# A transformer block on one core: every engine's parts put in another order, laid out with VectorE and GpSimd excluding each other

## The chip, the cores and the metric

The kernel runs on one core of a Trainium2 chip. The metric is the device time of one execution in microseconds. Before the change the median of three runs is 976.28 us (975.53 to 977.0). Engines are called by their short names: PE is TensorE (matmul), PEld its weight load, DVE VectorE, ACT ScalarE, POOL GpSimd, SP the engine that issues the DMAs.

## The reference

Sixteen sequences of 256 tokens with 128 features each pass through one block, all in float32. Cut to its steps:

```python
x = x + layernorm(attn_ref(layernorm(x)))   # 1: selective scan, an MLP, causal attention, an MLP
x = x + layernorm(ffn_ref(layernorm(x)))    # 2: gated feed-forward, hidden size 512
# attn_ref, for each sequence
vg = rms_norm(x) @ in_proj_w; value = silu(conv4(vg[:256])); gate = vg[256:]
Bm, Cm = x @ B_proj_w, x @ C_proj_w                   # 16 heads x 64
y = selective_scan(value, A, Bm, Cm, dt) + D * value  # decay of each head to the power (q - k)
x = x + (y * silu(gate)) @ out_proj_w;  x = x + relu(rms_norm(x) @ fc)**2 @ proj
q, k, v = ...; rms_norm and rope on q and k; softmax(q k / sqrt(8), causal) @ v   # 16 heads, 4 for k and v
x = x + att @ o_w;  x = x + relu(rms_norm(x) @ fc)**2 @ proj
# ffn_ref
h = silu(x @ w1) * (x @ w2); h = gelu(h @ h1); h = gelu(h @ h2); return h @ w3
```

## The kernel before

The program is written engine by engine. The work of one sequence `i` is cut into named parts, and each part is a small Python function that first waits for semaphores, then issues one to 48 instructions, and then raises its own semaphore. `PER` says how many instances of a part a sequence has. Sequences overlap: while one is in its scan, an earlier one is in attention and one before that in the feed-forward. Nothing is decided at run time. `ORDERS` (L48) is a table with one list of part names for each engine, `run` walks it, and each engine executes its list strictly in that order, so a part whose input is late holds up all that stands behind it on its engine.

The parts of PE and their instructions as the profile shows them: `tin` (transposes of `xm` and `X`), `inv` and `gat` (`w_in`), `bc` (`w_B`, `w_C`, eight of a sequence), `cb` (`BC` by `BC`, eight), `v` (`M,xpad`, four), `vt` (transposes of `val`), `out` (`w_out`), `up` and `down` (`w_mfc`, `w_mpj`), `t3` and `qkv` (`xa`, `w_qkv`), `qt`, `kt` (`Qs`, `Ks`), `s` (`KT,QT`), `mt` (`Mh`), `e` (`QT,KT`), `pv` (`PT,Va`), `yt`, `t4`, `o`, `t5`, `upb`, `downb` (`w_apj`), `t6`, `w1` and `w2` (`x6H`, `x6L`), `h1` and `h2` (`gH`, `gL` by `w_h`; 24 matmuls each instance, two of each), `w3` (`w` by `gAB`). Products that need float32 precision are split in a high and a low half (`xnH` and `xnL`, `x6H` and `x6L`, `gH` and `gL`).

Three forms of PE work matter below. Most parts use the array's 128 rows and 128 columns. `cb` works on 64 rows at a time (`64*128` in the profile). `v` and `pv` fill 32 columns each (`128*32`), `s` and `e` use 32 rows (`32*128`).

Around PE stand these parts. DVE: `nrm` (`X<-xm`, L932), `xnlo` (`xnL`, L937), `conv` (`val<-vpad`, L949 and L951), `m` (`M<-pool,LM`, L961 and L962), `nw`, `rp`, `qs` (normalisation and rope of q and k, L994 to L1057), `mx` (`mneg`, L1064), `mh`, and the layernorms. ACT: `bcx` (PSUM to `BC`), `ex` (exponential to `PT`), the activations. POOL: `sel` (the causal mask on `PT`), `sq` and `sqb` (squares), `glo` and `hlo` (low halves of the feed-forward), `xr`, and small powers `r1` to `r8`. The setup, once: `pex` on ACT and `plm` on DVE make the decay table `LM` (L579, L852); `plo` on DVE makes the low halves of `w_in`, `w_B`, `w_C` (L862, L865); `fsc` and `flo` on POOL scale and split the weights of the feed-forward (L414, L419, ten each of 128x512); `fold` on DVE folds scales into weights. The first `relu` waits for six `flo`, since `hid` holds raw weights until then.

PSUM has eight banks. `BANKS` gives each PE part its bank or banks, and `claim` waits for the part that last read a bank.

Of the kernel before, what the change touches and what calls it, by code (L numbers as in the profile page):

```python
# [1510 lines left out]
```

## Time and profile before

| | |
|---|---|
| median of 3 runs | 976.28 us |
| the profiled execution | 976.42 us, its span 974.7 us, mean granted clock 0.988 |
| PE busy | 888.5 us (91%), 9248 matmuls |
| DVE busy | 667.8 us (69%) |
| ACT busy | 578.2 us (59%) |
| POOL busy | 460.0 us (47%) |

The span runs from the first to the last instruction; 1.7 us of the profiled execution lie outside it. A busy share says how much an engine works, not whether its work is waited for. The page's chain of work that ended last is 64% PE, 22% DVE, 7% issue, 3% ACT, 2% POOL.

### The profile page before, as it was taken

What the parts mean: (1) busy time and instruction counts of PE and PEld (TensorE: products, weight loads), DVE (VectorE), ACT (ScalarE), POOL (GpSimd) and SP (SyncE); (2) the same over time, 40 slices, a digit from 0 to 9 for tenths busy, and PEclk for the clock granted to TensorE, in tenths of its full rate; (3) what the DMA queues carried; (4) which work ended last, traced back from release to release, by engine and by line L of the source; (5) the groups of instructions that cost most, each with busy time, mean ns of one, the idle gap of its engine ahead of it and who ended that gap; (6) DMA issues with size and microseconds to landing.
All of it is one profiled execution on the core that took longest, in us unless ns stands there. A gap on an engine that the chain in (4) does not pass through costs nothing.

```text
span 974.7 us, 24913 instructions
## 1 busy us (share of the span) xinstructions
PE 888.5 (91%) x9248; PEld 758.0 (78%) x9248; DVE 667.8 (69%) x1803; ACT 578.2 (59%) x1220; POOL 460.0 (47%) x708
## 2 busy tenths in 40 slices
PE   0689989999999999998999999999999999989785
PEld 0667768787979888987878898888877887878575
DVE  5978969866777767758576884875776686746320
ACT  3644365766747557746565768567475575575532
POOL 1574344625543637435345545355263644463432
PEclk9999999999999999999999999999999999999899
DMA  8100000000000000000000000000000000000000
GB/s 280 59 17 7 7 7 2 7 1 13 7 13 7 13 2 7 13 12 6 12 7 2 17 2 12 8 12 7 12 2 2 2 13 1 13 1 13 12 3 9
DMA packets 17926, 15.71 MB, mean 16 GB/s; under 512 B 2064, under 2 KB 15760, under 8 KB 17552
## 3 DMA queue, kind: packets, MB, share of 16 engines
q1 hardware_dynamic: 17808, 14.12, 4.6%
q8 instruction: 76, 1.25, 0.5%
q14 instruction: 42, 0.34, 0.1%
HBM read 12.02 MB, written 2.10 MB: 14 GB/s over the span
## 4 chain that ended last, share of the span: by engine, by line
PE 64%; DVE 22%; issue 7%; ACT 3%; POOL 2%; DMA 1%; SPq 0%; POOLq 0%; DVEq 0%; ACTq 0%
PE pool L1170 59%; PE pool L1187 5%; DVE mneg L1064 2%; DVE val L951 2%; DVE M L961 1%; DVE M L962 1%; ACT PT L726 1%; DVE W L1018 1%; DVE val L949 1%; DVE gAB L1144 1%; DVE W L1020 1%; POOL PT L496 1%; DMA X<-in_x 1%; DVE LM L852 1%; DVE val L968 1%
## 5 line engine op out<-in xcount | busy, mean ns | idle before, releaser
L1064 DVE TENSOR_REDUCE mneg<-pool 128x2 f32<-128x512 f32 (+1 forms) x192 | 119.0, 683 | 54.7 <-PE pool L1170 54.7
L1170 PE MATMUL pool<-gH,w_h_hi 128*128 128x256 f32 x512 | 149.1, 291 | 4.8 <-POOL gL L542 2.2
L1170 PE MATMUL pool<-gL,w_h_hi 128*128 128x256 f32 x512 | 143.8, 281 | 0.0
L1170 PE MATMUL pool<-gH,w_h_lo 128*128 128x256 f32 x512 | 143.8, 281 | 0.0
L961 DVE TENSOR_TENSOR M<-pool,LM 128x512 f32<-128x512 f32 x128 | 87.6, 685 | 55.2 <-PE pool L1170 54.8
L726 ACT ACTIVATE PT<-pool 128x512 f32<-128x512 f32 x192 | 99.2, 603 | 31.8 <-PE pool L1170 31.5
L1170 PE MATMUL pool<-BC 64*128 64x256 f32 (+1 forms) x1024 | 111.4, 345 | 3.3 <-ACT PT L726 1.7
L496 POOL TENSOR_SCALAR_AFFINE_SELECT PT<-PT 128x256 f32<-128x256 f32 (+1 forms) x192 | 89.2, 488 | 42.4 <-ACT PT L726 39.0
L1170 PEld LDWEIGHTS pool<-BC 64*128 64x128 f32 x1024 | 87.6, 187 | 26.1 <-issue 14.1
L644 ACT ACTIVATE BC<-pool 128x512 f32<-128x512 f32 x128 | 75.6, 603 | 54.2 <-PE pool L1170 50.9
L1170 PEld LDWEIGHTS pool<-gH,w_h_hi 128*128 128x128 f32 x512 | 96.9, 189 | 7.2 <-issue 3.2
L1170 PEld LDWEIGHTS pool<-gL,w_h_hi 128*128 128x128 f32 x512 | 97.0, 189 | 0.2
L1170 PEld LDWEIGHTS pool<-gH,w_h_lo 128*128 128x128 f32 x512 | 96.8, 189 | 0.0
L542 POOL TENSOR_TENSOR gL<-gAB,gH 128x512 fp32r<-128x512 f32 x32 | 41.3, 1301 | 65.2 <-ACT gH L787 64.9
L547 POOL TENSOR_TENSOR gL<-gAB,gH 128x512 fp32r<-128x512 f32 x32 | 41.0, 1286 | 50.1 <-ACT gH L801 50.0
L1170 PE MATMUL pool<-M,xpad 128*32 128x256 f32 (+1 forms) x1024 | 54.8, 332 | 3.6 <-DVE M L962 3.6
L1170 PE MATMUL pool<-PT,Va 128*32 128x128 f32 (+1 forms) x1024 | 53.2, 338 | 5.1 <-POOL PT L496 5.1
L806 ACT ACTIVATE gAB<-pool 128x512 f32<-128x512 f32 x32 | 19.1, 598 | 63.5 <-PE pool L1170 63.4
L951 DVE SCALAR_TENSOR_TENSOR val<-vpad,cols,val 128x256 f32<-128x256 f32 x96 | 54.9, 612 | 0.4
L962 DVE TENSOR_TENSOR M<-pool,LM 128x256 f32<-128x256 f32 x128 | 53.0, 414 | 0.0
L1170 PE MATMUL pool<-xnH,w_B_hi 128*128 128x256 f32 x128 | 44.0, 344 | 4.4 <-DVE M L962 3.9
L512 POOL TENSOR_TENSOR hid<-hid 128x512 f32<-128x512 f32 x32 | 33.5, 1051 | 29.7 <-ACT hid L766 29.7
(235 smaller groups left out, 2428.0 us busy)
## 6 DMA issues: line engine op xcount, KB each, us to landing
X<-in_x SPq DMA_DIRECT2D x16, 128.0 KB, 2.1
x<-in_x SPq DMA_DIRECT2D x16, 128.0 KB, 2.2
out<-ob SPq DMA_DIRECT2D x16, 128.0 KB, 2.1
hid<-in_w_h SPq DMA_DIRECT2D x1, 1024.0 KB, 8.9
gAB<-in_w_h SPq DMA_DIRECT2D x1, 1024.0 KB, 9.4
PT<-in_w_B SPq DMA_DIRECT2D x1, 512.0 KB, 4.9
PT<-in_w_C SPq DMA_DIRECT2D x1, 512.0 KB, 6.4
Qs<-in_s SPq DMA_DIRECT2D x1, 512.0 KB, 5.0
```

The source lines that it names most:

```text
L496: g.affine_select(w, w, pattern=[[0, w.shape[1]], [1, P]], compare_op=ALU.is_ge, fill=0.0, base=0, channel_multiplier=-1).then_inc(S["sel" ...
L512: g.tensor_tensor(h, h, h, ALU.mult).then_inc(S["sqb"], 1)
L542: g.tensor_tensor(gL[:, J], gA[:, J], gH[:, J].bitcast(F32), ALU.subtract).then_inc(S["glo"], 1)
L547: g.tensor_tensor(gL[:, J], gB[:, J], gH[:, J].bitcast(F32), ALU.subtract).then_inc(S["hlo"], 1)
L644: a.activation(BC[:, n % NBC, :], bank("bc", i, k), ACT.Copy).then_inc(S["bcx"], 1)
L726: a.activation(PT[:, n % NPT, :], bank("e", i, k // 4, k % 4), ACT.Exp).then_inc(S["ex"], 1)
L951: last = v.scalar_tensor_tensor(dst, vpad[:, b, k:k + L], w, dst, ALU.mult, ALU.add)
L961: v.tensor_tensor(M[:, n % NM, :, 0:L], pool8[:, b:b + 2, 0:L], LM[:, 2 * k:2 * k + 2, :], ALU.mult)
L962: v.tensor_tensor(M[:, n % NM, :, L:3 * P], pool8[:, b:b + 2, L:3 * P], LM[:, 2 * k:2 * k + 2, 0:P], ALU.mult).then_inc(S["m"], 1)
L1064: v.reduce_max(dst, o, axis=AX.X, negate=True).then_inc(S["mx"], 1)
L1170: return p.matmul(o, lhsT, rhs, start=start, stop=True, skip_group_check=True)
L1187: last = p.transpose(o[:, k * P:(k + 1) * P], src(k), ident[:])
```

## The change

All five lists of `ORDERS` and the table `BANKS` are replaced. The lists hold the same parts, the same number of each: no operand, shape or buffer changes. By its description the new order was laid out with DVE and POOL excluding each other wherever a DVE instruction has all its inputs in SBUF. One wait is added, on POOL in `xr`, for POOL's own part of the sequence before. Two lines are added, so every line after it stands two higher in the kernel after.

```diff
 ORDERS = dict(
     PE=(
-        "tin inv gat bc bc bc cb cb cb bc bc bc vt v cb cb bc v cb cb bc v cb tin v inv bc gat bc cb cb out bc bc bc vt t2 cb "
...
+        "tin inv bc bc bc gat bc bc cb cb bc bc cb cb vt bc v v cb cb cb cb v v tin bc inv out t2 up up bc bc bc down bc cb "
...
     DVE=(
-        "st0 dec ag0 st0 ag0 xh m01 dec xh dec plo dec xm dec plo dec nrm plo plm plm plm plm plm plm plm plm xnlo fold fold "
...
 BANKS = (
-    "0102314523016745023451234512312301234501231045123450230245234502012321024501236745012301452672014567201456201745"
...
+    "0102304567012345670124567014530123230230145204523674516730450267450360724523701745021374650127426375012567126735"
...
@@ -464,6 +464,8 @@
                 pool.wait_ge(S["xh"], at("xh", i))
                 g.tensor_tensor(xr[:, i % 2], xh[:, i % 2], by(R_A1), ALU.mult).then_inc(S["xr"], 1)
             elif k == 1:
+                if i >= 1:
+                    pool.wait_ge(S["xr"], at("xr", i - 1))
                 pool.wait_ge(S["xm2"], at("xm2", i))
                 g.tensor_tensor(xt[:], xm[:, i % 2], by(R_A0), ALU.mult).then_inc(S["xr"], 1)
```

What the tables do is seen in the instructions. The start on DVE, before, from the first `nrm` (`X<-xm`) on:

```order
L932 TENSOR_SCALAR X<-xm,rsd 128x128 x2
L865 TENSOR_TENSOR w_C_lo<-PT,w_C_hi 128x1024
L852 SCALAR_TENSOR_TENSOR LM<-LM,sc,xr 128x256 x16
L937 TENSOR_TENSOR xnL<-pool,xnH 128x512
L870 SCALAR_TENSOR_TENSOR t4s<-t4s,rows 128x128
L871 TENSOR_TENSOR w_out<-w_out,t4s 128x256
L872 TENSOR_TENSOR w_mpj<-w_mpj,t4s 128x512
L875 TENSOR_SCALAR t5s<-t5s 128x128
```

And after:

```order
L934 TENSOR_SCALAR X<-xm,rsd 128x128 x2
L867 TENSOR_TENSOR w_B_lo<-PT,w_B_hi 128x1024
L867 TENSOR_TENSOR w_C_lo<-PT,w_C_hi 128x1024
L939 TENSOR_TENSOR xnL<-pool,xnH 128x512
L854 SCALAR_TENSOR_TENSOR LM<-LM,sc,xr 128x256 x10
L872 SCALAR_TENSOR_TENSOR t4s<-t4s,rows 128x128
L873 TENSOR_TENSOR w_out<-w_out,t4s 128x256
L874 TENSOR_TENSOR w_mpj<-w_mpj,t4s 128x512
L951 TENSOR_SCALAR val<-vpad,cols 128x256 x2
```

`xnL`, for which PE's first real matmul waits, stood behind all 16 instructions that build `LM`; now it stands ahead of them, and ten of them follow it, two more come after the first `conv`, and the last four stand ahead of the second `M`.

The first sequence's scan on PE, before (`BC` by `BC` is `cb`, `M,xpad` is `v`):

```order
L1187 MATMUL pool<-ident,val 128x128 x4
L1170 MATMUL pool<-M,xpad 32x256 x4
L1170 MATMUL pool<-M,xpad 32x128 x4
L1170 MATMUL pool<-BC 128x256 x2
L1170 MATMUL pool<-BC 128x128 x2
L1170 MATMUL pool<-BC 128x256 x2
L1170 MATMUL pool<-BC 128x128 x2
L1170 MATMUL pool<-xnH,w_B_hi 128x256
```

And after:

```order
L1172 MATMUL pool<-M,xpad 32x256 x4
L1172 MATMUL pool<-M,xpad 32x128 x4
L1172 MATMUL pool<-M,xpad 32x256 x4
L1172 MATMUL pool<-M,xpad 32x128 x4
L1172 MATMUL pool<-BC 128x256 x2
L1172 MATMUL pool<-BC 128x128 x2
L1172 MATMUL pool<-BC 128x256 x2
L1172 MATMUL pool<-BC 128x128 x2
L1172 MATMUL pool<-BC 128x256 x2
L1172 MATMUL pool<-BC 128x128 x2
L1172 MATMUL pool<-BC 128x256 x2
L1172 MATMUL pool<-BC 128x128 x2
```

Before, each `v` is followed by two `cb` and then full-array work; after, two `v` and four `cb` stand together. Over the whole of PE's two lists a `cb` follows a `cb` 32 times before and 50 times after, and neighbours of unlike form stand next to each other 468 times before and 436 times after.

The end on PE, before, around the last sequence's `t3` and `qkv` (`ident,xa` and `w_qkv,t3s`; `w_mpj,hid` is its `down`, `PT,Va` and `QT,KT` are `pv` and `e` of the one before):

```order
L1170 MATMUL pool<-w_mpj,hid 128x128 x8
L1187 MATMUL pool<-ident,xa 128x128 x2
L1187 MATMUL pool<-ident,x2n 128x128 x2
L1170 MATMUL pool<-PT,Va 32x256 x8
L1170 MATMUL pool<-QT,KT 128x512 x4
L1170 MATMUL pool<-w_qkv,t3s 128x192 x2
L1170 MATMUL pool<-x6H,w_hi 128x256
L1170 MATMUL pool<-x6L,w_hi 128x256
L1170 MATMUL pool<-x6H,w_lo 128x256
```

And after:

```order
L1172 MATMUL pool<-x6L,w_hi 128x256
L1172 MATMUL pool<-x6H,w_lo 128x256
L1189 MATMUL pool<-ident,xa 128x128 x2
L1172 MATMUL pool<-PT,Va 32x128 x16
L1172 MATMUL pool<-w_qkv,t3s 128x192 x2
L1189 MATMUL pool<-ident,yv 128x128 x4
L1189 MATMUL pool<-ident,ytm 128x128 x2
L1172 MATMUL pool<-gH,w_h_hi 128x256
L1172 MATMUL pool<-gL,w_h_hi 128x256
```

Before, `qkv` of the last sequence has an earlier sequence's `w2` and then `h2` behind it; after, all four `w1` and `w2` of that sequence stand ahead of `t3`, and `yt`, `t4` and `h1` follow `qkv`. Between the last `qkv` and the next part of that sequence (`qt` or `kt`) PE's list holds 2 `w2`, 2 `h2`, 1 `pv`, 1 `w3`, 1 `yt`, 2 `w1` and 1 `t4` before, and 1 `yt`, 1 `t4`, 2 `h1` and 1 `o` after.

## Rows read from the trace of the kernel before

**Rows 1.** Windows: stretch, length, busy (instructions) of PE, PEld, DVE, ACT, POOL; clock; DMA
```profile
0.00:97.50 97.50, 60.34 (x529) 51.39 (x530) 71.74 (x191) 46.70 (x109) 47.64 (x67) 0.96 0.28 91
97.50:195.00 97.50, 90.26 (x1042) 72.83 (x1040) 82.46 (x212) 56.10 (x130) 46.46 (x74) 1.00 0.02 6
195.00:864.00 669.00, 652.90 (x6904) 558.91 (x6902) 476.65 (x1289) 425.39 (x887) 322.17 (x502) 0.99 0.03 8
864.00:974.70 110.70, 84.97 (x777) 74.82 (x776) 36.94 (x115) 50.03 (x96) 43.72 (x66) 0.96 0.03 8
```

**Rows 2.** Waits of TensorE, 0 to 97 us: total, times, longest
```profile
PE pool L1187 <- DVE X L932: 22.5, 2, 21.6
PE pool L1170 <- DVE xnL L937: 7.0, 1, 7.0
PE pool L1170 <- DVE M L962: 6.5, 4, 3.9
```

**Rows 3.** Waits of TensorE, 97 to 864 us
```profile
PE pool L1187 <- DVE Qs L1057: 3.5, 3, 1.3
```

**Rows 4.** Waits of TensorE, 864 us to the end
```profile
PE pool L1170 <- POOL PT L496: 3.9, 3, 2.7
```

**Rows 5.** Timeline of TensorE: start us, us, engine, line, tiles, count
```profile
35.12 2.23 PE L1170 MATMUL pool<-BC 64*128 64x256 f32 x24
...
49.56 0.92 PE L1170 MATMUL pool<-BC 64*128 64x256 f32 x8
50.41 0.44 PE L1187 MATMUL pool<-ident,xm 128*128 128x128 f32 x2
```

**Rows 6.** Groups by form, TensorE, 195 to 877 us: count, busy us, mean ns
```profile
L1170 PE MATMUL pool<-xnH,w_B_hi 128*128 128x256 f32 x87 | 30.4, 350 | 0.4 <-DVE QT L1081 0.4
...
L1170 PE MATMUL pool<-xnL,w_B_hi 128*128 128x256 f32 x87 | 24.5, 281 | 0.0
```

**Rows 7.** Timeline of GpSimd, 36 to 61 us
```profile
37.46 2.83 POOL L414 TENSOR_TENSOR PT<-PT,Qs 128x512 f32<-128x512 f32 x2
...
54.74 5.43 POOL L419 TENSOR_TENSOR w_h_lo<-hid,w_h_hi 128x512 fp32r<-128x512 f32 x4
```

**Rows 8.** Timeline of VectorE, 37 to 41 us
```profile
37.81 2.56 DVE L932 TENSOR_SCALAR X<-xm,rsd 128x128 f32<-128x128 f32 x2
```

**Rows 9.** Timeline of VectorE, beside GpSimd's setup
```profile
56.31 5.55 DVE L951 SCALAR_TENSOR_TENSOR val<-vpad,cols,val 128x256 f32<-128x256 f32 x4
61.78 0.68 DVE L961 TENSOR_TENSOR M<-pool,LM 128x512 f32<-128x512 f32 x1
```

**Rows 10.** Groups by form, VectorE, whole span: count, busy us, mean ns
```profile
L961 DVE TENSOR_TENSOR M<-pool,LM 128x512 f32<-128x512 f32 x128 | 87.6, 685 | 55.2 <-PE pool L1170 54.8
...
L951 DVE SCALAR_TENSOR_TENSOR val<-vpad,cols,val 128x256 f32<-128x256 f32 x96 | 54.9, 612 | 0.4
...
L892 DVE BATCH_NORM_STATS2 bst<-X 128x6 f32<-128x128 f32 x32 | 7.6, 279 | 10.4 <-DMA X<-in_x 10.4
```

**Rows 11.** Timeline of all engines, 20 to 30 us
```profile
21.03 0.47 DVE L932 TENSOR_SCALAR X<-xm,rsd 128x128 f32<-128x128 f32 x2
...
21.42 1.22 DVE L865 TENSOR_TENSOR w_C_lo<-PT,w_C_hi 128x1024 fp32r<-128x1024 f32 x1
...
22.56 6.41 DVE L852 SCALAR_TENSOR_TENSOR LM<-LM,sc,xr 128x256 f32<-128x256 f32 x16
...
28.89 0.68 DVE L937 TENSOR_TENSOR xnL<-pool,xnH 128x512 fp32r<-128x512 f32 x1
```

**Rows 12.** Timeline of TensorE, the last sequence
```profile
868.54 0.89 PE L1170 MATMUL pool<-w_qkv,t3s 128*128 128x192 f32 x4 [0.33 <-DVE x6L L1138]
...
882.45 1.09 PE L1187 MATMUL pool<-ident,Qs 128*128 128x128 f32 x8
```

**Rows 13.** Timeline of TensorE: one `h1` part, from its first matmul to the next part
```profile
400.91 0.28 PE L1170 MATMUL pool<-gH,w_h_hi 128*128 128x256 f32 x1
...
403.73 0.38 PE L1187 MATMUL pool<-ident,ytm 128*128 128x128 f32 x2
```

More of the change, by code:

```diff
@@ L49 @@
     PE=(
[26 rows of a table removed]
[26 rows of a table added]
     ),
     Activation=(
-        "pxx phi phi ss1 phi pex pex pex pex pex pex pex pex xnhi va ga bcx bcx bcx ss1 bcx bcx val fhi bcx xp fhi fhi fhi "
-        "fhi bcx fhi fhi bcx fhi fhi xnhi fhi va bcx ga bcx bcx val bcx bcx xp t2c ss2 bcx bcx bcx relu relu ss1 ss3 t3c qk "
-        "xnhi vv ss2 va t2c bcx bcx bcx val ga bcx xp bcx bcx ss1 relu relu ktc qtc ss3 bcx bcx qtc t3c qk xnhi va bcx bcx ga "
[9 rows of a table removed]
-        "bcx ghi ghi val yv relu xp bcx ge1 t4c ktc qtc hhi ge1 ss4 hhi t5c qtc relu relub ge2 ge2 relub bcx bcx bcx ex ex ex "
[8 rows of a table removed]
@@ L99 @@
-        "ga xp ge2 ss2 ge2 t2c bcx ss1 bcx bcx bcx bcx ktc qtc qtc ss4 relu relu t5c xnhi relub va relub ga bcx bcx val ss2 "
[7 rows of a table removed]
+        "pxx phi phi ss1 phi xnhi pex pex pex pex bcx pex pex pex va ga bcx bcx bcx bcx ss1 pex val fhi fhi bcx xp bcx bcx "
+        "fhi xnhi fhi fhi fhi fhi t2c fhi bcx relu fhi relu bcx ss2 va bcx ss3 t3c bcx val fhi qk xp bcx vv bcx ss1 bcx bcx "
[12 rows of a table added]
+        "hhi ktc bcx hhi bcx qtc ss4 val qtc t5c relub relub relu xp ss1 ge2 ge2 bcx bcx bcx ex ex xnhi bcx ex ex t3c ss3 ex "
[4 rows of a table added]
@@ L107 @@
+        "t5c ge1 hhi hhi relub relub ge2 ge2 ktc qtc qtc xnhi ss2 va t2c bcx bcx ga bcx bcx relu t6hi bcx relu bcx val sl sl "
+        "xp ss1 ex ex ex ss3 ex t3c ex ex ex ex bcx bcx qk ex ex ex ex ghi ghi xnhi yv vv va ge1 bcx ge1 hhi hhi bcx bcx ga "
+        "t4c bcx ktc val qtc ge2 ge2 xp ss2 bcx t2c ss1 bcx bcx bcx qtc t5c xnhi ss4 relub relub relu relu ss2 va t2c ex bcx "
[7 rows of a table added]
     ),
     DVE=(
-        "st0 dec ag0 st0 ag0 xh m01 dec xh dec plo dec xm dec plo dec nrm plo plm plm plm plm plm plm plm plm xnlo fold fold "
[34 rows of a table removed]
+        "dec st0 ag0 dec dec plo m01 xh xm dec dec dec nrm plo plo xnlo plm plm plm plm plm fold conv plm st0 m ag0 conv fold "
[34 rows of a table added]
@@ L144 @@
     ),
     Pool=(
-        "zero r1 r1 r1 r1 r2 r2 xr r2 r2 fsc fsc fsc fsc fsc fsc fsc fsc fsc fsc flo flo gp flo flo flo flo flo xr flo xr xr "
-        "flo flo zero sq sq r3 r1 r3 r1 r1 r1 r2 r2 r4 gp r4 xr r3 xr xr r3 r2 r2 sq sq r1 r1 r4 r4 gp xr r3 xr xr r3 sq sq "
-        "r1 r1 sel sel sel sel r2 r2 sel sel sel sel sel sel sel sel r1 r1 gp xr xr r3 r3 r5 r5 sqb sqb r2 r2 r6 r6 x1 xr r7 "
-        "r7 sel sel sel sel r4 r4 sel sel sel sel sq sq sel sel sel sel gp glo glo xr r3 xr r3 r1 r2 r1 r2 r5 r5 hlo hlo sqb "
@@ L150 @@
-        "sqb r8 r8 outp r6 sel sel r6 sel sel x1 r7 r7 xr r4 r4 sel sel sel sel sel sel sel sel glo glo sq sq gp r1 r1 hlo r5 "
-        "r5 xr hlo xr r3 r3 r2 r2 sqb sqb r8 r8 outp r6 r6 x1 sel sel sel sel r7 r7 xr r4 r4 sel sel sel sel sq sq sel sel "
-        "sel sel glo glo r1 r1 hlo hlo r5 r5 gp xr r8 xr r8 sqb r3 outp sqb r2 r3 r2 sel sel sel sel r6 r6 sel x1 sel sel sel "
-        "r7 r7 xr r4 r4 sel sel sel sel glo glo sq r5 r5 gp hlo hlo sqb xr sqb xr r3 r3 r6 r6 sel sel x1 sel sel r7 r7 r2 r2 "
@@ L168 @@
-    SP=(
-        "loadx loadx loady loady loadx loadx loadx loadx loady store loadx loady store loadx loady store loadx loady store "
-        "loady store loadx loady store loadx loady store loadx loady store loadx loady store loadx loady store loady store "
+        "zero r1 r1 r2 r2 r1 r1 r2 xr r2 fsc fsc fsc fsc fsc flo fsc fsc flo flo fsc fsc flo gp flo flo xr flo sq sq fsc r3 "
[7 rows of a table added]
+        "sel r4 r4 sel sel xr sel sel r1 r1 glo glo r2 sq sq sel sel sel sel hlo hlo sqb sqb outp r8 r5 r5 r8 r3 r6 r6 x1 sel "
@@ new lines @@
+        "sel outp r7 r7 sel sel sel sel sel sel r4 r4 gp sel sel sel sel r1 glo xr glo xr hlo hlo sqb xr r3 sq sq r2 r5 r3 r2 "
[6 rows of a table added]
+        "sel glo glo r3 hlo r3 hlo r5 r5 sqb xr sqb r8 r8 gp sel sel sel r6 r6 sel sel sel xr xr sel sel r4 x1 sel sel r7 r7 "
+        "sel sel r4 glo r3 glo sq r3 sqb sqb r5 r5 hlo hlo outp r6 r6 sel sel sel sel sq x1 r7 r7 sel sel sel sel sel xr sel "
+        "r4 sel sel r4 glo glo r8 r8 gp r5 sqb sqb r5 xr hlo hlo xr outp r6 r6 sel sel sel sel x1 sq sq r7 r7 r3 sel r3 sel "
@@ new lines @@
+        "sel sel sel sel sel sel r4 r4 r8 r8 glo glo hlo hlo sqb sqb r5 r5 r8 outp r8 sel sel sel r6 r6 x1 sel sel sel r7 r7 "
+        "sel sel sel sel sel sel glo glo outp hlo sqb sqb r5 r5 hlo r6 r6 x1 r7 r7 r8 r8 glo glo hlo hlo outp r8 r8 outp"
+    ),
+    SP=(
+        "loadx loadx loady loady loadx loadx loadx loady store loadx loadx loady loadx store store loady loadx store loady "
+        "loady store loadx loadx loady store loadx loady store store loady loady store loadx loadx loady store store loady "
@@ L187 @@
-    "4510232012301230167452301674523012345670124670154206754207450450145261761452761045267103452673201456701234567020"
-    "14560214543056305217634254107652341012576342301574602120123010123001010203101010"
+    "0102304567012345670124567014530123230230145204523674516730450267450360724523701745021374650127426375012567126735"
+    "0123672350671203671031431367014523676760176045023176452361475236745231674235641723256741354067453067454035670345"
+    "1672016726012745601267450126701452601456012467012546701546735343014056756012345674564567401467230145146723456714"
@@ new lines @@
+    "5672345236542023230134576201345671245067312452067423670230672306236705230152367051260167523015267340102304567120"
+    "3456731204167423067420672341231607142367401421367240136701524362012347562341257634012641723645123623456017067236"
+    "4521030457620145761204501674034106753014657340134601572045710450124573163016036701453467013246375012460137340167"
+    "3470136267014236740160274567456072450267340523016742301367420153670421320156742056237516742135673245674526745221"
+    "0123014506731245670321465031203403501674325016734256710341567315367301301034567310145301670170451762345162364730"
@@ L189 @@
+    "2451630674513203124567312067231456723243567435673451676124567012301204567301023456723245672345167231456723024524"
+    "5670132637450162345701623745127614523167236701236752352360175263275601273501235367015345670132453067136457301450"
+    "1230263701230145623013425601342546012354601235460234502310452301432560126456201452601245017652401203476501247356"
+    "40127367012012101230167451230671452012036741523617452313412101023001010123401010"
 )
```

17 lines of the change are left out of this document (removed), and 183 rows, old and new, of tables (Activation, DVE, PE, Pool).

## The prediction

> **What bounds the kernel now.** I read the windows first, then PE's waits in three stretches, then timelines of the start and the end. The windows [rows 1] give PE's idle time as length less busy: 37.2 us in the first 97.5 us, 7.2 us up to 195 us, 16.1 us in the 669 us up to 864 us, and 25.7 us in the last 110.7 us, together 86.2 us of 974.7 us. In the long middle PE is busy 97.6%, so there the order can win two things only: fewer of the 16.1 us, and less PE work. More than two thirds of the idle time lies at the two ends, where one sequence's chain of dependent parts runs with little beside it.
>
> At the start PE waits 21.6 us for `X`, 7.0 us for `xnL`, and then 6.5 us in four waits for `M`, the longest 3.9 us [rows 2]. In the middle the largest releaser, `Qs`, holds only 3.5 us in three waits [rows 3]. At the end the waits are spread over `PT`, `x6L`, `hid`, `gL`, the largest 3.9 us in three [rows 4].
>
> **Whether VectorE and GpSimd exclude each other here.** They do, for some instructions. Two `X<-xm` on VectorE take 2.56 us from 37.81 us on [rows 8], while GpSimd runs two multiplications from 37.46 us to 40.29 us [rows 7]; at 21.03 us, with GpSimd idle, the same two took 0.47 us [rows 11]. Four `conv` steps take 5.55 us [rows 9] beside four `flo` of 5.43 us [rows 7], 1.39 us each, as long as one `flo` (1.36 us). The next instruction, `M<-pool,LM`, reads PSUM and takes its usual 0.68 us [rows 9, 10]. Over the whole span a `conv` step has a mean of 612 ns [rows 10]. The 16 `LM` instructions, of the same form and with GpSimd idle, take 6.41 us or 400 ns each [rows 11], so the lock costs up to 96 x 0.21 = 20 us on `conv` alone. VectorE is 69% busy, so only the part of this that sits just ahead of something PE wants is on the path.
>
> The layout's rule is wider than what the trace shows. `bst<-X`, a statistic whose one input lies in SBUF, has a mean of 279 ns [rows 10], no trace of a lock. The Trainium skill, page "SBUF — State Buffer", section "Who interferes with whom", names as contenders VectorE instructions with two SBUF inputs (against GpSimd instructions that read SBUF) and those in a two-port mode, and leaves the rest free. The trace agrees on all three kinds of row. By it the new order keeps some statistics and aggregates away from GpSimd for nothing; that is one of the rivals below.
>
> **The change part by part.** The sum is made against the profiled execution, 976.42 us with a span of 974.7 us.
>
> *PE's work.* No matmul is added, but changing the form of work costs time. Three `cb` in a row take 2.23 us, one alone 0.92 us [rows 5], so each following one adds (2.23 - 0.92) / 2 = 0.655 us; a lone one holds PE for 50.41 - 49.56 = 0.85 us until the next part starts. Entering `cb` from other work costs 0.20 us. Going back to the full array costs something too: the first matmul of a `bc` has a mean of 350 ns, its third kind 281 ns [rows 6]. 37 of the 128 `bc` in PE's list follow a split form, so if all of the 69 ns lies there, a return costs 0.069 / 0.29 = 0.24 us; a lower bound is 0.10 us, half an entry. I take 0.18 us. Counting neighbours in PE's two lists: entries to `cb` fall from 96 to 78, returns to the full array from 171 to 162, entries to `v` or `pv` from 106 to 101 (0.17 us each, my estimate between the two others). That is 18 x 0.20 + 9 x 0.18 + 5 x 0.17 = 6.1 us less PE work, with bounds of 3 and 8 us (32 changes fewer at 0.10 and at 0.24). About a fifth of it falls at the two ends, where PE waits anyway. I take -5 us.
>
> The Trainium skill, page "TensorEngine Tiling (Array Packing)", section "Key Properties", says that changing the tiling mode, not merely the tile, drains TensorE. The 0.20 us agree with it. If the changes cost nothing this term would be 0 and my forecast 5 us higher.
>
> *The start.* Before, `xnL` stands behind the 16 `LM` instructions; it starts at 28.89 us, and they take 6.41 us [rows 11]. After, it stands directly behind the two `lo` products of 1.22 us each, one of which ran earlier before. So PE's first products start 5 to 6 us sooner, at about 24 us. But the `LM` instructions now stand between `xnL` and the `M` that need them, and VectorE, busy 71.7 of the first 97.5 us with its input not there for the first 12 [rows 1], has hardly a gap there. From `xnL` to the eighth `M` its list now has 6.4 us more of `LM` work, and 0.5 us more of statistics. What PE gains at `xnL` it waits again at `v`, which needs `M`. Then the first `down` stands much earlier in PE's list, behind 24 us of PE work where it stood behind 38. It needs `hid`, and the first `relu` needs GpSimd's sixth `flo`. Nine `fsc` and seven `flo` at 1.36 to 1.41 us [rows 7], 22 us in all, one gate product and one `xt` (2 us, an estimate from the same rows by size) stand ahead of its two squares (2 us likewise). From 37.5 us on that gives 63.5 us for the start of `down`. The two effects cancel within a microsecond or two. I take -1 us; the bounds are -6 (all of the earlier `xnL` kept) and +6 (`down` waits as long as the 7.0 us wait it replaces).
>
> *The middle.* The idle time from 97.5 to 864 us is 23.3 us. I compared, part by part, how much PE work (each part at its usual time in the trace) stands in the two lists between a part and the next one of the same sequence that needs its result by way of VectorE or GpSimd. That distance is longer after for the links with VectorE instructions that the lock can stretch or that stand behind such: from `bc` to its `cb` the lower quarter goes from 2.3 to 3.6 us, from `cb` to its `v` from 2.2 to 2.8 us, from `inv` to `vt` from 8.1 to 10.7 us; from `e` to the first `pv`, through GpSimd's masks, from 4.2 to 5.0 us. The links shorter than the bare latency that the trace shows are as few after as before. So waits caused by late VectorE results should shrink. They can't shrink by more than the 23.3 us; I take -5 us, with bounds of -15 and +8, since a list on ACT or VectorE that holds a late part ahead of a needed one is not seen in such distances.
>
> *The end.* From the last `qkv` at 868.54 us to the next part of that sequence at 882.45 us [rows 12] VectorE works through `nw`, `rp` and `qs`. Before, PE's list has 2 `w2`, 2 `h2`, 1 `pv`, 1 `w3`, 2 `w1` and smaller parts there, and PE was busy nearly throughout. After, it has 2 `h1` (2.82 us each [rows 13]) and about 1.1 us of small parts, 6.8 us of work under a chain of 13.2 us: a new hole of about 6 us. Against it, PE has done 11 us more of its list when it comes to that `qkv`, so less is left: 63.5 us of work instead of 74.8, counted in the lists with each part's usual time. Further on, between the last `mt` and `e`, the list has 5 us of work where it had 10, under a chain of some 13 us. Taking the chain from the last `down` to the end as 108 us (110.7 us before, two microseconds less for work it no longer waits behind) over 72 us of remaining work instead of 77.5, PE idles 36 us there by the same reckoning that gives 33 before. I take +3 us; bounds -5 and +7.
>
> *The added wait* on GpSimd is for GpSimd's own earlier instructions in the same list, done before it is reached. It costs 0.
>
> Sum: -5 - 1 - 5 + 3 = -8 us, so 976.4 - 8 = 968.4; the median lay 0.1 us below the profiled execution, so 968 us.
>
> **The rivals.** *Switches only:* the middle keeps its 23.3 us of waits, because PE hardly waited for locked instructions there [rows 3], and the end takes 3 us back. Then -5 + 3 = -2 us and the start within 1 us: 974 us. What speaks for it is how little idle time the middle has. A layout rule wider than the lock gives this too.
>
> *The middle loses most of its waits:* with longer distances everywhere, 15 of 23.3 us go and the end gives 1: -5 - 1 - 15 + 3 = -18, or 958 us. The distances speak for it; against it, no releaser in the middle holds more than 3.5 us [rows 3], so there is no one cause whose removal would give it.
>
> *Slower: the early `down`.* PE's list now brings the first `down` up when GpSimd is still in its setup, and all of PE stands behind it. If the mutual lock stretches GpSimd's setup, or `relu` comes late on ACT's list, `down` starts later than 68 us instead of 63; from there on every microsecond is lost. At 70 us that is +7 us, with the end at its bound of +7, the middle unchanged and -5 for the switches: +9, so 985 us. Against it: in the trace it is VectorE that is stretched beside GpSimd's 1.36 us instructions, not GpSimd.
>
> **How the numbers follow.** My forecast of 968 us has 0.45 (its own range 962 to 973), switches only 0.23 (974, from 972 to 978), the large gain 0.17 (958), slower 0.15 (985). A difference of 0.2% (2.0 us) is about what a measurement of this kernel can tell from none: faster is below 974.3 us, slower above 978.2 us. Faster is 0.45 + 0.17 and half of the switches-only case, 0.74; same is the rest of it, 0.11; slower 0.15. The range of 956 to 980 us leaves out part of the first and most of the last case.
>
> **What would show it.** The windows of the changed kernel should give a PE idle time of 35 to 38 us in the first 97.5 us and 25 to 30 us in the last 110. PE's busy time should fall by 5 to 6 us. The first matmul on `xnH` should start near 24 us with a wait of 1 to 3 us instead of 7.0, and the waits for `M` in the first 97 us should rise above 6.5 us. The first `down` should start near 63 us. Between the last `qkv` and `qt` there should be one wait of 5 to 7 us for `Qs` or `Ks`. I am wrong if PE's busy time doesn't fall, if the middle's idle time rises above 25 us, or if the first `down` starts after 68 us.

## The result and the profile after

The changed kernel takes 942.6 us in the median of four runs (942.0 to 944.6) where the kernel before takes 975.9 us (975.5 to 977.0): a ratio of 0.966, 95% interval 0.964 to 0.968. I had said 968 us and 956 to 980 us, so the direction was right and the size wrong by a factor of four. The profiled span falls from 974.7 to 940.3 us, by 34.4 us.

The windows of the changed kernel, to be laid against [rows 1]; the last line covers its last 110.7 us, the length of the last stretch of before:

```profile
0.00:97.50 97.50, 66.82 (x619) 55.55 (x623) 70.99 (x202) 48.27 (x109) 43.86 (x64) 0.91 0.27 91
97.50:195.00 97.50, 95.64 (x1078) 79.66 (x1078) 80.38 (x214) 60.93 (x140) 46.20 (x75) 1.00 0.02 5
195.00:864.00 669.00, 660.88 (x7100) 571.18 (x7092) 479.12 (x1324) 422.35 (x909) 333.93 (x523) 1.00 0.03 8
829.60:940.30 110.70, 89.40 (x820) 78.29 (x818) 39.37 (x129) 55.08 (x102) 51.07 (x80) 0.94 0.04 11
```

PE's idle time (length less busy) is 30.7 us at the start, 1.9 and 8.1 us in the middle (before 7.2 and 16.1), 21.3 us at the end. The counts say more than the idle time: in the 766.5 us from 97.5 to 864 us PE runs 7946 matmuls before and 8178 after.

PE's waits, 0 to 97 us after (total, times, longest), against [rows 2]:

```profile
PE pool L1189 <- DVE X L934: 14.7, 1, 14.7
PE pool L1189 <- DVE M L964: 5.4, 1, 5.4
PE pool L1172 <- DVE xnL L939: 3.2, 2, 1.8
PE pool L1172 <- DVE M L964: 2.5, 2, 1.2
PE pool L1172 <- ACT xpad L639: 2.2, 1, 2.2
```

From 97 to 864 us, against [rows 3], and from 864 us on, against [rows 4], the largest ones are:

```profile
PE pool L1189 <- DVE ytm L1095: 2.1, 3, 0.9
...
PE pool L1172 <- POOL PT L498: 3.0, 2, 2.7
```

In the middle `Qs` is gone from the list. One view that I had not used says more. It is the page's part 4, the chain that ended last, by engine; first before, then after:

```profile
PE 64%; DVE 22%; issue 7%; ACT 3%; POOL 2%; DMA 1%; SPq 0%; POOLq 0%; DVEq 0%; ACTq 0%
```

```profile
PE 51%; DVE 3%; issue 2%; POOL 1%; ACT 1%; DMA 0%; POOLq 0%; ACTq 0%; DVEq 0%
```

These two don't compare as they stand: the chain of after is followed back only to 387.7 us, and so its shares reach 58%. Over the same stretch, 387.7 to 864 us, VectorE holds 81.3 us of the chain before and 25.2 us after (its pieces added up), 17% and 5%. Its busy time fell as well, from 667.8 to 650.5 us, with the same 1803 instructions.

**A measure for what follows.** Idle time hides a wait that is counted as part of a matmul. So I use PE's delay: the time at which a part of PE's list ended, less the usual durations (from the trace of before, by kind and by whether the form changes) of all parts up to it. A program works it out from the trace; no view of the profile shows it. The list holds 851.2 us of work before and 844.7 us after. Delays in us, at four points of that work:

```
order, run            at 15   at 60  at 790    end
before                 33.6    44.5    95.0  117.8
after                  33.1    42.4    69.4   89.9
after, second run      33.5    42.3    69.2   93.0
after, third run       34.0    42.7    69.8   91.7
```

The 34.4 us are: 6.5 less work, 2.1 won up to 60 us of work, 23.5 won between 60 and 790 us (before loses 50.5 there, after 27.0), 2.3 won behind that. The last is no finding: three executions of the same changed kernel differ by 3 us there. How much is called work and how much delay hangs on what is taken as usual: with durations from the lower fifth to the lower third of each kind, the middle comes out at 27 to 29 us and the work at 1.5 to 3.4 us. That the middle gave most of it holds either way. Of the 50.5 us of before, 27.0 lie in 27 delays of at least 0.6 us; after has ten such, of 8.2 us together.

### The profile page after: what moved, and what is told of

It reads as the page before. It is cut to its first block, busy times and chain, and to the rows that moved or that the text cites. A ratio compares the mean times of both kernels' runs of the same rounds, so it can differ in the third digit from the quotient of the medians.

```text
span 940.3 us, 24915 instructions
## 1 busy us (share of the span) xinstructions
PE 879.4 (94%) x9248; PEld 755.8 (80%) x9248; DVE 650.5 (69%) x1803; ACT 561.6 (60%) x1211; POOL 454.6 (48%) x708
## 4 chain that ended last, share of the span: by engine, by line
PE 51%; DVE 3%; issue 2%; POOL 1%; ACT 1%; DMA 0%; POOLq 0%; ACTq 0%; DVEq 0%
PE pool L1172 46%; PE pool L1189 4%; DVE mneg L1066 1%; DMA X<-in_x 0%; ACT PT L728 0%; POOL gL L549 0%; POOL hid L514 0%; DVE val L951 0%; DVE gAB L1146 0%; DVE bst L894 0%; ACT gH L803 0%; ACT BC L646 0%; DVE val L970 0%; DVE val L953 0%; POOL x L529 0%
## 5 line engine op out<-in xcount | busy, mean ns | idle before, releaser
L1066 DVE TENSOR_REDUCE mneg<-pool 128x2 f32<-128x512 f32 (+1 forms) x192 | 119.8, 682 | 43.2 <-PE pool L1172 43.0
L728 ACT ACTIVATE PT<-pool 128x512 f32<-128x512 f32 x192 | 102.9, 602 | 25.5 <-PE pool L1172 25.0
L1172 PE MATMUL pool<-BC 64*128 64x256 f32 (+1 forms) x1024 | 108.5, 345 | 2.2 <-ACT BC L646 1.3
L953 DVE SCALAR_TENSOR_TENSOR val<-vpad,cols,val 128x256 f32<-128x256 f32 x96 | 52.0, 583 | 0.5
L1172 PEld LDWEIGHTS pool<-M,xpad 128*32 128x32 f32 x1024 | 27.7, 111 | 25.5 <-DVE M L964 6.1
```

Of the source, the lines that this page charges most:

```text
L728: a.activation(PT[:, n % NPT, :], bank("e", i, k // 4, k % 4), ACT.Exp).then_inc(S["ex"], 1)
L953: last = v.scalar_tensor_tensor(dst, vpad[:, b, k:k + L], w, dst, ALU.mult, ALU.add)
L1066: v.reduce_max(dst, o, axis=AX.X, negate=True).then_inc(S["mx"], 1)
L1172: return p.matmul(o, lhsT, rhs, start=start, stop=True, skip_group_check=True)
```

## The experiments

Theory A: the time came from VectorE instructions that GpSimd no longer stretches just ahead of something PE wants. Rival B: dependent parts stand further apart, whatever the stretching. Rivals C and D are on the start: C, the earlier statistics gave much of it; D, other parts bind there.

**One input instead of two, in both orders.** The arithmetic is left out, so these kernels don't compute the block; the parts, their order and their waits stay:

```
+        def one_input(dst, src):
+            return v.reduce_sum(dst, src.unsqueeze(len(src.shape)), axis=AX.X)
-   last = v.scalar_tensor_tensor(dst, vpad[:, b, k:k + L], w, dst, ALU.mult, ALU.add)
+   last = one_input(dst, vpad[:, b, k:k + L])
-   one = v.tensor_tensor(Wk(1), Wk(3), gain[:], ALU.mult)
+   one = one_input(Wk(1), Wk(3))
...
```

> The order of before, with the four steps of each convolution, the normalisation steps (all but the subtraction that reads PSUM) and one sum of the rotary part replaced on VectorE by a reduction with one input of the same size: that arithmetic is left out, the parts, their order and their semaphores stay. Theory A (the delays in the middle are VectorE instructions stretched while GpSimd runs): most of what those instructions take above their shortest goes, about 50 of the 71 us that all such VectorE instructions take over their shortest in the profile of before, and with it some 20 to 25 us of the 50 us by which TensorE falls behind its work between 60 and 790 us of work: about 952 us. Theory B (the order of before puts dependent parts too close, whatever the stretching): VectorE's busy time falls but TensorE's delays stay, 970 to 976 us.

> The same replacement in the order of after, the same arithmetic left out. Theory A: the order has already kept the stretching off the path (TensorE falls behind by 27 us between 60 and 790 us of work, against 50), so little is left to win: 934 to 940 us, and the distance of the two orders shrinks from 33 us to 12 to 20 us (6 of them TensorE's own work, the rest start and end). Theory B: the distance stays near 33 us, 940 to 943 us here against 970 to 976 us with the order of before.

> The order of before with only the four steps of each convolution replaced on VectorE by a reduction with one input of the same size (that arithmetic is left out); the normalisation steps and the rotary sum stay as they were. Before to this kernel with all of them replaced was 23 us (ratio 0.976). If the convolutions carry most of it, since they stand between TensorE's projections and its transposed values: 957 to 962 us. If the normalisation steps of the attention (9.5 us of stretching in the profile of before, 2.6 us in that of after) carry it, 968 to 974 us.

> The order of before, with the normalisations (X, xh, xm, l, x2n and the two of the output) and the last step of Ks and Qs replaced as well by a reduction with one input of the same size, on top of the convolution and the normalisation steps of the attention; all of that arithmetic is left out. If the 11 us that are left in the middle are more stretching: TensorE falls behind by about 26 to 29 us between 60 and 790 us of work instead of 34.0 us, and the time falls by 4 to 8 us, a ratio to before of 0.969 to 0.973. If they are the distances: the ratio stays within 0.975 to 0.978.

> The same in the order of after, the same arithmetic left out. Either way little is left there: within 3 us of the run with one input in the order of after, a ratio to before of 0.956 to 0.960. The distance of the two orders is then 10 us or less if it was stretching, and 16 to 19 us if it was the distances.

```
order, run             ratio to before        at 15  at 60  at 790    end
before, conv only      0.983 (0.981-0.985)    33.0   37.3    77.6  102.2
before, one input      0.976 (0.973-0.980)    33.4   37.6    71.6   96.0
before, more of them   0.970 (0.966-0.974)    33.5   36.5    65.3   88.1
after, one input       0.959 (0.956-0.962)    33.1   41.0    63.8   86.6
after, more of them    0.958 (0.954-0.961)    32.7   41.5    63.6   86.6
```

With nothing in the order changed, the kernel before gets 23 us faster by this, and 29 us with more instructions replaced; the order of after gets 7 and 8 us faster. The two orders are 33 us apart as they are, 17 us, then 12 us (for the last I had said 10 us or less if it was stretching, 16 to 19 us if it was the distances: it lies between). Between 60 and 790 us of work the distance goes from 23.5 us to 11.2 and then to 6.7 us (28.8 against 22.1). So the stretching is what the order of before pays for, and rival B as I put it, whatever the stretching, has 6.7 us left (10 to 13 us with the other choices of the usual durations), not all of it surely B's: the last step of `rp` and the `Mh` instructions kept two inputs. The `conv` steps alone carry 17 of the 23 us, about 7 of them within the first 60 us of work and 10 in the middle.

Two things limit this. The stand-in is not only free of stretching, it is also shorter: 0.41 us where an unstretched `conv` step with two inputs takes 0.48 us, 6.6 us over the 96 of them. The order of after has the same saving and gains 7 us in all. And the runs don't say in which way the new order escapes the stretching. Of the 128 `conv` steps 28 take more than 0.6 us before and 24 after, 76.8 us together before and 71.0 us after, where 59.2 us would be unstretched: two thirds of the stretching are still there. (All VectorE instructions together stand 77 us above the shortest of their kinds before and 56 us after.) What changed is how long before its use `val` is ready. Before, PE's `vt` starts at most 1.6 us after ScalarE ends `val` in 15 of 16 sequences; after, it starts 2.8 to 11.9 us later in 8 of 16. One of them, VectorE, ScalarE and TensorE after:

```profile
377.90 1.91 DVE L953 SCALAR_TENSOR_TENSOR val<-vpad,cols,val 128x256 f32<-128x256 f32 x2
379.85 0.63 ACT L629 ACTIVATE val<-val 128x512 f32<-128x512 f32 x1
391.25 0.60 PE L1189 MATMUL pool<-ident,val 128*128 128x128 f32 x4
```

The two steps are stretched to 0.95 us each, and PE does not wait for `val`. So a third reading stands untested: dependent parts further apart let the stretching pass unseen. No run keeps one of the two, fewer stretched instructions or longer distances, and takes the other away.

The place of the largest single delay in the middle shows how the stretching costs time before. VectorE:

```profile
451.94 2.71 DVE L951 SCALAR_TENSOR_TENSOR val<-vpad,cols,val 128x256 f32<-128x256 f32 x2
454.58 1.03 DVE L1018 SCALAR_TENSOR_TENSOR W<-W 128x40 f32<-128x40 f32 x1
455.53 0.87 DVE L951 SCALAR_TENSOR_TENSOR val<-vpad,cols,val 128x256 f32<-128x256 f32 x2
```

GpSimd beside it:

```profile
451.92 1.04 POOL L476 TENSOR_TENSOR hid<-hid 128x512 f32<-128x512 f32 x1
452.92 1.45 POOL L542 TENSOR_TENSOR gL<-gAB,gH 128x512 fp32r<-128x512 f32 x1
454.33 1.22 POOL L476 TENSOR_TENSOR hid<-hid 128x512 f32<-128x512 f32 x1
```

And TensorE, which needs that `val`:

```profile
453.09 1.58 PE L1170 MATMUL pool<-BC 64*128 64x256 f32 x16
457.11 1.11 PE L1187 MATMUL pool<-ident,val 128*128 128x128 f32 x4 [2.44 <-ACT val L627]
...
459.09 0.41 PE L1170 MATMUL pool<-gH,w_h_hi 128*128 128x256 f32 x1
...
460.26 0.28 PE L1170 MATMUL pool<-gH,w_h_hi 128*128 128x256 f32 x1
```

Two `conv` steps take 2.71 us while GpSimd has three instructions running, and 0.87 us once it has none. `val` comes late, PE waits 2.44 us, and then the clock is granted at the lower level for a while (0.79 in the mean from 455 to 463 us): the same matmul takes 0.41 us, later 0.28 us. The wait is put down to ScalarE, which only passes the lateness on; the cause is two steps back. The same place in the run with one input, VectorE and then TensorE:

```profile
438.48 0.73 DVE L817 TENSOR_REDUCE val<-vpad 128x256 f32<-128x256 f32 x2
```

```profile
440.66 1.58 PE L1173 MATMUL pool<-BC 64*128 64x256 f32 x16
442.17 0.66 PE L1190 MATMUL pool<-ident,val 128*128 128x128 f32 x4
```

No wait, and no lower clock behind it (1.00 from 195 to 864 us).

**More changes of form on TensorE.**

```
+        if a[0] == b[0] == "cb" and after[0] in small:
+            order[x + 2], order[x + 3] = after, b
```

> The order of after with pairs of cb on TensorE taken apart, so that one of the 15 kinds of part with small matmuls stands between them: 50 changes of form more on TensorE (486 instead of 436), everything else in its order. By the price that I read from before (0.18 to 0.20 us for each change of form) TensorE's work grows by 9 us and so does the time, to 951 to 953 us; since some parts move by one place, up to 2 us of waits either way. If the changes of form cost nothing and the 6 us of TensorE's busy time had another source: within 1.5 us of the changed kernel.

> The changed kernel itself once more, unchanged, as the measure for the other kernels of this call on the same chip. Its ratio to before was 0.966 with an interval of 0.964 to 0.968: the same is expected again, 942 to 944 us where before takes 976.

955.8 us against 944.7 us for the changed kernel on the same chip: 11.1 us for 50 changes, 0.22 us each. The delay stays (43.2 at 60 and 70.6 us at 790 us of work, against 42.3 and 69.2), so it is work and no waits. The price that I took, 0.17 to 0.20 us, was a little low; 32 changes fewer are worth 7 us if those at `v` and `pv`, which this run does not add to, cost as much.

**The start: the statistics of the second sequence.** VectorE's `st0` and `ag0` of the second sequence behind the first `nrm` in the order of before, or in front of it again in that of after:

```
+    place("DVE", ('st0', 1, 0), ('nrm', 0, 0))    # in before, with ag0, xh, and r1 on Pool
+    place("DVE", ('st0', 1, 0), ('ag0', 0, 0))    # in after, with ag0
```

> The order of before with one thing done: VectorE's statistics of the second sequence (and GpSimd's part that needs them) stand behind the first normalisation instead of ahead of it. In the profile of before the first normalisation waits there for the second sequence's transfer and begins at 21.03 us, in that of after at 14.05 us. Theory C (the start gives a good part of the 33 us): the first projection begins about 7 us earlier and the time falls by 3 to 6 us, to 970 to 973 us. Theory D (the first 60 us are set by GpSimd's set-up and the first masks, since TensorE's lag at 40 us of work is 40.7 us before and 40.5 us after): the first products come 7 us earlier, wait for M, and the time changes by less than 1.5 us, 974.5 to 976.5 us.

> The order of after with the second sequence's statistics put back in front of the first normalisation on VectorE. Theory C: 3 to 6 us slower, 946 to 949 us. Theory D: the first normalisation begins near 19 to 21 us instead of 14 us, the first M follows by about as much less its wait, and the time rises by 0 to 2 us, 942.5 to 944.5 us.

In the order of before the move gives 2 us (ratio 0.998, 0.996 to 1.000), 1.3 us of them still there at 60 us of work: nearer to D. In the order of after the move back costs 4 to 6 us (0.970, 0.967 to 0.973, where the changed kernel has 0.964 to 0.966), and the delay at 60 us of work is 7.2 us more: theory C there. Nearly the same move (that in before takes GpSimd's `r1` and VectorE's `xh` along) is worth 2 us in one order and 5 us in the other. My reading, not tested: in before GpSimd's setup and the stretched `conv` are late too.

**The start: freeing what PE waits for.** Four edits of the order of after; `place` puts a part behind another one.

```
e11:  Activation: pex 7 behind pex 6
e7:   e11's; Activation: val 0 ahead of the copies; DVE: m 0.1 behind m 0.0, conv 2 and 3 and m 0.2 earlier, folds later
e8:   e7's;  Pool: r2 1.0, xr 0.0, r2 1.1 behind fsc 3
e10:  e11's; Activation: xp 0 behind val 0; DVE: m 0.1 behind conv 0.3
```

> The order of after with its first 60 us arranged anew on ScalarE and VectorE: the last exponential of the parameters stands with the other seven, so that two loads of ScalarE's function table go (near 31 and 33 us in the profile of after), the first val stands ahead of the remaining copies, and on VectorE the second and third M follow the first, with the folds of the later blocks behind them. In the profile of after TensorE waits 2.2 us for xpad, 1.1 us for val, 5.4 and 2.5 us for M in this stretch. If these waits are each set by what stands ahead of the part in its engine's order, 3 to 6 us faster, 937 to 940 us. If the start is set by GpSimd's set-up (it begins at 36.14 us, and the first down at 63.09 us is its consumer), within 1 us of the changed kernel.

> The same as the kernel ahead of it, and on GpSimd three parts for the second sequence and for the residual of the first moved behind the set-up of the mixing matrices, so that this set-up begins near 28 us instead of 36.14 us. If GpSimd's set-up is what the start waits for, 5 to 8 us faster than the changed kernel, 935 to 938 us. If VectorE's and ScalarE's parts are: the same time as the kernel ahead of it within 1 us; and if the parts moved back are needed at once (the second sequence's statistics), 1 to 3 us slower than that.

> The order of after with three parts moved in the first 40 us: on ScalarE the last exponential stands with the other seven (two loads of the function table go) and the first xpad copy stands right behind val instead of behind copies that wait for GpSimd's set-up; on VectorE the second M stands right behind the convolution's last step instead of behind the masks and a fold. In the profile of after TensorE waits 5.4 us for that M and then 2.2 us for xpad, and the v that needs xpad ends at 40.38 us. If the head of each engine's order is what delays the start: 3 to 5 us faster than the changed kernel, a ratio to before of 0.960 to 0.962 (937 to 940 us). If GpSimd's set-up, which ends near 51 us, sets it all the same, the gain comes back as waits behind it: within 1.5 us of the changed kernel, a ratio of 0.964 to 0.967.

> The order of after with the last exponential alone moved next to the other seven on ScalarE. ScalarE's loads at L581 and L629 (near 31.1 and 33.3 us, 1.3 us each) go, so val comes up to 2.6 us earlier; TensorE waits then for M (5.4 us before vt), which does not move: within 1 us of the changed kernel. If ScalarE's val is what vt waits for, 2 us faster.

None of them gained: 0.969, 0.969, 0.966 and 0.964 for e7, e8, e10 and e11, where the changed kernel gives 0.964 to 0.966; e7 and e8 are 5.0 and 4.4 us slower than it on the same chip. For e7 I had allowed no loss over 1 us; e8 within 1 us of e7, e10 within 1.5 us and e11 within 1 us of the changed kernel were cases that I had named. e7, e8 and e10 remove a wait that they aim at and meet another one; e11 was not aimed at one. In e10 the M comes early and `xpad` follows at once, but the next BC copies still stand behind the weight copies that wait for GpSimd's setup, and PE waits 6.4 us for one of them. In e7 ScalarE is held by those copies ahead of `xpad` (7.0 us).

**The whole chain at once.** What holds GpSimd's setup is read from its own row, after:

```profile
34.80 0.73 POOL L465 TENSOR_TENSOR xr<-xh,rows 128x256 f32<-128x256 f32 x1 [3.15 <-DVE LM L854]
```

`xr` overwrites what VectorE's last parameter products read. So VectorE's products, GpSimd's `xr` and setup, ScalarE's weight copies and then the BC and `xpad` copies form one chain. The edits:

```
+    place("Activation", ('pex', 7, 7), ('bcx', 0, 4))
+    place("Activation", ('xp', 0, 0), ('val', 0, 0))      # then bcx 0.5, bcx 0.6
+    place("DVE", ('m', 0, 1), ('conv', 0, 3))              # then plm 6, plm 7
 e13 only:
+    place("Pool", ('r2', 1, 0), ('fsc', 3, 3))             # then xr 0.0, r2 1.1
```

> The order of after with seven parts moved in its first 45 us. ScalarE: the last exponential stands ahead of the second sequence's sum of squares, and the xpad copy and the next two BC copies stand right behind val, ahead of the copies that wait for GpSimd's set-up. VectorE: the second M and then the last two parameter products stand right behind the convolution, ahead of two folds. GpSimd's order stays; its xr waits for those parameter products (3.1 us until VectorE's LM at L854 in the profile of after). One-chain theory: v0 starts near 36 us instead of 40.4 us, no wait for xpad or BC over 1 us, GpSimd's set-up begins up to 1 us earlier, and the kernel is 2 to 5 us faster than the changed one (a ratio to it of 0.995 to 0.998). Rival (GpSimd's set-up is what everything behind it waits for, and it is not moved): the time is the same within 1 us, and the wait comes back ahead of up or down near 60 us.

> The same, and GpSimd's three parts for the second sequence stand behind the first four parts of its set-up, so that the set-up runs beside the convolution on VectorE from about 29 us. If the stretching of VectorE's convolution is what this costs, its four steps at L953 take 3 to 4 us where they take 1.9 us in after, val comes 1.5 to 2 us later, and the kernel is 0 to 2 us slower than e12. If the set-up's start is what the first 60 us hang on: 3 to 6 us faster than e12.

> The changed kernel itself, unchanged, as the measure for the two ahead of it on the same chip: a ratio to before of 0.964 to 0.967, and a first v that ends near 41.9 us, as in its first profile.

e12 takes 941.4 us against 943.5 us for the changed kernel on the same chip, a gain of 2.2 us, likely and not sure: the spreads hardly meet (940.3 to 941.8, 941.7 to 945.5), though the ratios to before, 0.962 and 0.964, overlap in their intervals. Its delay is 39.4 us at 60 us of work instead of 42.4 to 42.7 us and keeps that lead to 790 us (66.0 against 69.8). It is the fastest order that I ran with all the arithmetic in. TensorE in e12, first `vt` and the first two `v`:

```profile
32.45 0.66 PE L1208 MATMUL pool<-ident,val 128*128 128x128 f32 x4 [2.39 <-ACT val L648]
34.38 1.48 PE L1191 MATMUL pool<-M,xpad 128*32 128x256 f32 x16 [0.56 <-ACT BC L665]
40.62 1.51 PE L1191 MATMUL pool<-M,xpad 128*32 128x256 f32 x16 [4.77 <-DVE M L983]
```

The same in after:

```profile
35.80 1.09 PE L1189 MATMUL pool<-ident,val 128*128 128x128 f32 x4 [5.36 <-DVE M L964]
40.38 1.51 PE L1172 MATMUL pool<-M,xpad 128*32 128x256 f32 x16 [2.21 <-ACT xpad L639]
43.12 1.51 PE L1172 MATMUL pool<-M,xpad 128*32 128x256 f32 x16 [1.23 <-DVE M L964]
```

The first `v` starts 6.0 us earlier, and 4.8 us of that are waited for at the second, whose `M` stands behind the two stretched `X<-xm`. The setup did not begin earlier: `xr` now runs beside VectorE's casts and takes 1.65 us instead of 0.73 us.

e13 is 3 us slower than the changed kernel and 5.5 us slower than e12. VectorE there, beside GpSimd's setup (29.66 to 35.04 us), and then the same instructions in e12:

```profile
29.70 1.78 DVE L903 TENSOR_TENSOR w_apj<-w_apj,t5s 128x512 f32<-128x512 f32 x1
31.40 2.50 DVE L929 TENSOR_SCALAR xh<-X,mv,rsd 128x128 f32<-128x128 f32 x2
33.93 1.38 DVE L951 TENSOR_TENSOR xm<-xh,rows 128x256 f32<-128x256 f32 x1
35.24 1.78 DVE L975 SCALAR_TENSOR_TENSOR val<-vpad,cols,val 128x256 f32<-128x256 f32 x4
```

```profile
27.92 0.69 DVE L900 TENSOR_TENSOR w_apj<-w_apj,t5s 128x512 f32<-128x512 f32 x1
28.52 0.60 DVE L926 TENSOR_SCALAR xh<-X,mv,rsd 128x128 f32<-128x128 f32 x2
29.15 0.43 DVE L948 TENSOR_TENSOR xm<-xh,rows 128x256 f32<-128x256 f32 x1
29.50 1.79 DVE L972 SCALAR_TENSOR_TENSOR val<-vpad,cols,val 128x256 f32<-128x256 f32 x4
```

I expected the stretching on `conv`; it fell on the three instructions ahead of it, 5.66 us instead of 1.72, and `conv` began when the setup paused. The effect on `val` was larger than I said, since it ran 5.6 us later than in e12 and not 2. Here an idle GpSimd beside a busy VectorE was worth more than an early setup.

## Why the prediction was wrong

*PE's work, -5 us: right in size.* 32 changes of form fewer at the measured 0.22 us are 7 us, of which some lie at the ends; the measure above gives 6.5 us, and 1.5 to 3.4 us with the other choices of the usual durations. The test that I named for it was a poor one. PE's busy time fell by 9.1 us, but in the order of before it falls by 8.1 us (888.5 to 880.4) by the one-input instructions alone, with no form changed: the busy time also holds stretches at the lower clock and waits inside matmuls.

*The start, -1 us: right in size (-2.1), wrong in its working.* I let the first products start at about 24 us; they start at 17.54 us. I had missed that VectorE's list held the second sequence's statistics ahead of the first `nrm`, although [rows 10] give 10.4 us of idle time ahead of `bst<-X` for the transfer; after, it is 1.4 us. I had also given PE 35 to 38 us of idle time in the first 97.5 us, and it had 30.7 us. VectorE after:

```profile
14.05 0.47 DVE L934 TENSOR_SCALAR X<-xm,rsd 128x128 f32<-128x128 f32 x2
...
16.71 0.69 DVE L939 TENSOR_TENSOR xnL<-pool,xnH 128x512 fp32r<-128x512 f32 x1
```

That the gain at `xnL` is waited for again at `M` held: 7.9 us of waits for `M` [rows 2 had 6.5], and the first `down` starts at 63.09 us where I said 63.5. That this came so close is in part luck: GpSimd's setup began at 36.14 us and not at 37.5 us and its 16 instructions took 1.26 us each and not 1.38 us, but 3.1 us of waits, which I had not counted, stand between them and ahead of the squares:

```profile
63.09 2.01 PE L1172 MATMUL pool<-w_mpj,hid 128*128 128x128 f32 x16
```

*The middle, -5 us: the step that failed.* This term measured -23.5 us between 60 and 790 us of work. The mechanism was the one that I named, waits caused by late VectorE results. Its size was wrong twice. First, nothing led from the longer distances to the 5 us, and the idle time alone fell by more: from 97.5 to 864 us it went from 23.3 to 10.0 us, by 13.3 us. Second, the sentence "They can't shrink by more than the 23.3 us" took idle time for all that can be lost. In that stretch PE fell behind by 45.9 us before, twice its idle time there, and by 27.1 us after, so 5.5 of the 18.8 us won there lay within busy time. Lower clock is at most 4 us of that (granted clock 0.98 from 400 to 500 us and 0.97 from 800 to 864 us before, 1.00 after); for the rest I have only a guess, waits within the modelled ends of pipelined matmuls.

I also argued from the largest releaser, 3.5 us [rows 3], that there was no one cause. There was one, spread over many releasers, since a stretched `conv` shows as a wait for `val`, `M`, `BC` or `Qs`, whichever comes last. The chain's 22% for VectorE pointed to the larger gain. So did the up to 20 us that I worked out for `conv`, though that figure was itself misread: I set the mean duration of a stretched step, 612 ns, against 6.41 us / 16 = 400 ns from start to start. Set against the mean duration of one `LM` instruction, 476 ns, it is 96 x 0.136 = 13 us. The run with one input in `conv` alone gains 17 us, about 10 of them in the middle. The rival with 958 us had the right sign but the same cap (and its sum kept +3 us for the end where its text says 1).

*The end, +3 us: wrong.* There is no hole behind the last `qkv`. The next part of that sequence starts 8.7 us later, not 13.9 us as in [rows 12], and PE spends most of that in its two `h1`. TensorE after:

```profile
847.88 0.92 PE L1172 MATMUL pool<-w_qkv,t3s 128*128 128x192 f32 x4
...
856.58 0.65 PE L1189 MATMUL pool<-ident,Qs 128*128 128x128 f32 x4
```

I had taken 13.2 us as the length of that chain. But in before VectorE idled 4.29 us inside it, between the last `W` step and the rotary part. The rotary part waits for ScalarE's `Va`, and that stood on ScalarE's list behind two `gAB` instructions, each of which waited for PE. VectorE, then ScalarE, before:

```profile
874.00 0.20 DVE L1010 TENSOR_TENSOR W<-W,gain 128x40 f32<-128x40 f32 x1
878.50 0.49 DVE L1030 TENSOR_TENSOR ro<-pool,cosT 128x320 f32<-128x320 f32 x1 [4.29 <-ACT Va L703]
```

```profile
873.70 0.60 ACT L806 ACTIVATE gAB<-pool 128x512 f32<-128x512 f32 x1 [1.73 <-PE pool L1170]
876.52 0.60 ACT L806 ACTIVATE gAB<-pool 128x512 f32<-128x512 f32 x1 [2.22 <-PE pool L1170]
877.64 0.83 ACT L703 ACTIVATE Va<-pool,rsd 128x32 f32<-128x32 f32 x4 [0.53 <-PE pool L1170]
```

After, `Va` runs at 850.98 us, ahead of these, and the rotary steps stand between the `W` steps. A distance in time between two dependent parts is an upper bound of the latency, and I used it as the latency. Of PE's idle time in the last 110.7 us I had said 25 to 30 us; it was 21.3 us.

*The rivals and the two rules.* The case "slower" (a late `down`) did not come: `down` was on time. That a change of tiling mode costs TensorE time, as the Trainium skill has it on the page "TensorEngine Tiling (Array Packing)", section "Key Properties", agrees with the 0.22 us for each change; that the cost is a draining, no run here shows. The Trainium skill's rule on who contends (page "SBUF — State Buffer", section "Who interferes with whom") also agrees: the statistics, which have one input, keep a mean of 279 ns and `M<-pool,LM`, one of whose inputs is in PSUM, one of 685 ns, before and after.

## What to carry to other kernels

Idle time is not the most that better ordering can win: count how far the bounding engine falls behind the sum of its work, and read the engines' shares of the chain of waits before you cap a gain (over the same stretch, where you compare two chains). Measure stretching duration against duration. Where two engines stretch each other, what counts is the stretched time just ahead of something the bound engine wants, and it shows under the name of whoever comes last. A wait removed at the start of a program is worth only the distance to the next one: four edits of single waits gained nothing here, and moving the whole chain gained 2 us.

## What the hardware showed unexpectedly

- The stretching goes both ways. GpSimd's `xr` takes 0.73 us alone and 1.65 us beside VectorE's casts and one two-input multiplication (e12); I had held that only VectorE is stretched.
- It does not need two tensors: two `X<-xm` take 0.47 us alone and 2.51 us beside GpSimd's setup (after), two `xh<-X` 0.60 us alone (e12) and 2.50 us beside it (e13). Both have one tensor and scalars by partition.
- PE's waits in the start are followed by the lower of the two clock levels: from 34 to 47 us the granted clock is 0.50 after and 1.00 before (whose PE was busy 10.95 of those 13 us, against 7.75). Eight `BC` matmuls take 0.93 us at 25.17 us and 1.65 us at 44.56 us.
- A last exponential placed behind another function on ScalarE costs two table loads of 1.28 us; taking them away (e11) changed nothing measurable (0.964 with and without).
